# GNN with two residual norms: variances of four node groups on ScalarE, Newton steps a group later, 32 slot lookups moved on GpSimd

## What is computed

```python
# graph attention, 8 heads of 32 features
h = x @ W;  e = leaky_relu(a_src[src] + a_dst[dst], 0.2)
alpha = softmax of e over the edges with the same dst
g = relu(segment_sum(h[src] * alpha, dst) + bias)
x1 = layernorm(x + g)
# three convolutions with a batch norm each
y = x1
for l in range(3):
    e = relu((y[dst] - y[src]) @ theta[l].T + y[src] @ phi[l].T)
    agg = segment_max(e, src), 0 where a node has no edge
    y = relu((agg - mean(agg)) * rsqrt(var(agg) + 1e-5) * gamma[l] + beta[l])
out = layernorm(x1 + y)
```

## Time and profile before

| what | before |
|---|---|
| median of 3 runs | 1826.77 us (1820.73 to 1829.75) |
| the profiled execution, its own time | 1819.43 us |
| its span, first to last instruction | 1817.7 us |
| busy: PE / DVE / ACT / POOL | 1146.8 / 1262.6 / 997.6 / 973.9 us |
| mean granted TensorE clock | 0.811 |
| GAT stage, VectorE, groups 4 to 28 | to 404 us |
| softmax and groups 29 to 39, VectorE | 404 to 537 us |
| message stage and x1 scatters | 537 to 714 us |
| convolution 0, 1, 2 | 714 to 997, 997 to 1255, 1255 to 1460 us |
| last, dense stage | to the end |

### The profile page before, as it was taken

How to read it: one execution, slowest core, us unless ns; L and a number is a source line. 1 busy time by engine, 2 the same in 40 slices (tenths; PEclk the granted TensorE clock), 3 DMA queues, 4 the chain that set the end, 5 groups by cost and what they waited for, 6 DMA issues and landing times.

```text
span 1817.7 us, 16814 instructions
## 1 busy us (share of the span) xinstructions
PE 1146.8 (63%) x3863; PEld 584.4 (32%) x3863; DVE 1262.6 (69%) x2733; ACT 997.6 (55%) x2650; POOL 973.9 (54%) x1032
## 2 busy tenths in 40 slices
PE   0148888870029991899998599997999988000000
PEld 0023333320004441455554355543554444000000
DVE  8847777769979992354544255463766678989998
ACT  4736877765446763334443355553555544756664
POOL 1057767677767667777772777622644237640000
PEclk9999999985555555899999799998999999555555
DMA  9276899987775662688886366865866359999999
GB/s 366 110 219 220 288 330 367 365 273 250 221 283 143 214 208 96 198 258 258 263 260 184 77 180 184 169 171 126 150 130 136 105 160 299 418 402 383 385 378 371
DMA packets 177390, 436.11 MB, mean 240 GB/s; under 512 B 28804, under 2 KB 108810, under 8 KB 157324
## 3 DMA queue, kind: packets, MB, share of 16 engines
q1 hardware_dynamic: 109020, 229.52, 36.1%
q0 software_dynamic: 44800, 100.49, 22.0%
q10 hardware_dynamic: 23472, 105.03, 16.0%
HBM read 257.16 MB, written 182.32 MB: 242 GB/s over the span
## 4 chain that ended last, share of the span: by engine, by line
PE 29%; DVE 22%; DMA 20%; POOL 12%; issue 9%; ACT 7%; SPq 1%; ACTq 0%; POOLq 0%; DVEq 0%
PE ps L1247 10%; PE ps L1260 9%; DMA out<-arena 8%; DMA arena<-x 5%; POOL arena L1199 4%; POOL arena L1218 4%; DVE stat L782 3%; ACT arena L821 3%; DMA x<-big,idx 3%; PE ps L1237 3%; POOL slot L679 3%; PE ps L1424 2%; DVE arena L779 2%; DVE arena L1043 2%; DVE big L1052 2%
## 5 line engine op out<-in xcount | busy, mean ns | idle before, releaser
L1332 DVE TENSOR_TENSOR_SCAN arena<-arena,ps 128x512 f32<-128x512 f32 x150 | 191.0, 1277 | 263.6 <-PE ps L1247 241.8
L836 POOL DMA_INDIRECT arena<-x,idx x200 | 189.7, 948 | 172.7 <-DVE idx L603 90.9
L1218 POOL DMA_INDIRECT arena<-agg,slot x200 | 189.0, 945 | 171.4 <-PE ps L1237 72.3
L1247 PE MATMUL ps<-arena 128*128 128x512 f32 x600 | 277.0, 605 | 3.8 <-DVE arena L1332 3.8
L1260 PE MATMUL ps<-arena 128*128 128x512 f32 x600 | 273.4, 599 | 8.9 <-ACT arena L1302 8.9
L1199 POOL DMA_INDIRECT arena<-x,idx x200 | 189.2, 946 | 62.0 <-issue 58.5
L1529 ACT ACTIVATE ps<-arena 128x256 f32<-128x256 f32 x391 | 143.6, 367 | 100.9 <-DVE arena L1501 100.9
L821 ACT ACTIVATE arena<-arena,shift,inv 128x256 f32<-128x256 f32 (+1 forms) x311 | 156.0, 586 | 51.4 <-DVE shift L813 34.6
L1336 DVE TENSOR_TENSOR ps<-arena,ps 128x512 f32<-128x512 f32 x150 | 103.9, 695 | 107.2 <-PE ps L1260 107.2
L1302 ACT ACTIVATE arena<-big,bn_shift,bn_scale 128x512 f32<-128x512 f32 x100 | 75.9, 806 | 165.1 <-PE ps L1260 154.0
L1260 PEld LDWEIGHTS ps<-arena 128*128 128x128 f32 x600 | 115.2, 192 | 154.1 <-issue 144.7
(11 more groups left out here) (213 smaller groups left out, 2236.2 us busy)
## 6 DMA issues: line engine op xcount, KB each, us to landing
arena<-x SPq DMA_DIRECT2D x39, 1280.0 KB, 9.9
out<-arena SPq DMA_DIRECT2D x39, 1280.0 KB, 12.5
arena<-x ACTq DMA_DIRECT2D x31, 1280.0 KB, 10.5
x<-arena ACTq DMA_DIRECT2D x31, 1280.0 KB, 6.5
agg<-arena SPq DMA_DIRECT2D x50, 512.0 KB, 4.2
arena<-not_same SPq DMA_DIRECT2D x75, 256.0 KB
arena<-last_of SPq DMA_DIRECT2D x75, 256.0 KB
x_dst<-arena SPq DMA_DIRECT2D x25, 512.0 KB, 4.8
```

Of the source, the lines that this page charges most:

```text
L836: pl.indirect_dma_start(rows_in[:, par, a, g, :], None, x[:, :], bass.IndirectOffsetOnAxis(ap=idx[:, k, t * G + g:t * G + g + 1], axis=0)) ...
L1218: pl.indirect_dma_start(conv_in[:, b, 1, g, :], None, agg_dram[l - 1][:, :], bass.IndirectOffsetOnAxis(ap=slot[:, t * G + g:t * G + g + 1] ...
L1247: m = pe.matmul(far_bank[j], thp[:, l, 0, k, j * P:(j + 1) * P], far_t[:, par, k, :], start=(k == 0), stop=(k == 1))
L1332: v.tensor_tensor_scan(runmax[:, par, j, :], mask[:, tl % 2, :], far_bank[j], initial, ALU.add, ALU.max).then_inc(s_conv_scan, 1)
```

## The change

It has three parts. (1) Groups 29, 31, 33 and 35: VectorE no longer takes statistics; `pre_sums` adds the bias row by row with a fused instruction that also gives the row sum (ten instructions and one for the mean), and ScalarE's `pre_squares` takes ten squares of the differences from the mean, with their sums accumulated, into unused PSUM banks, ahead of the root. The other groups, and the tail, keep `pre_stats`. (2) From group 29 on VectorE does the sums or statistics of group g and then the Newton steps of g - 1, and ScalarE the root of g and then the turnover of g - 1. (3) SLOTS_TAIL = 3: only 12 lookups stay in front of the x1 scatters; the 32 others stand behind convolution 0's gathers, before the wait for the aggregates. A doubled definition, of which only the second was in use, goes too.

```diff
--- before.py
+++ after.py
@@ -672,6 +672,7 @@
             s(v.tensor_reduce(tiles_f[:, :], node_end, AX.X, ALU.add))
             s(v.tensor_scalar(tiles_needed[:, :], tiles_f[:, :], 1.0, None, ALU.add))
 
+        SLOTS_TAIL = 3
         SLOTS_EARLY = 11
         SLOTS_STEPS = 7
 
@@ -686,7 +687,7 @@
                 pl.indirect_dma_start(slot_dram[:, :], bass.IndirectOffsetOnAxis(ap=idx[:, S_END, c:c + 1], axis=0),
                                       slot_of_pos[:, c:c + 1], None, bounds_check=N - 1, oob_is_err=False).then_inc(s_slot_put, 16)
             pl.wait_ge(s_slot_put, 16 * NC)
-            for c in range(SLOTS_EARLY * G):
+            for c in range(SLOTS_TAIL * G):
                 slot_lookup(pl, c, s_slot_got)
 
 
@@ -765,11 +766,45 @@
             return 5 * g if g <= PRE_SORT else 5 * PRE_SORT + 4 * (g - PRE_SORT)
 
         def rbias_dve(v):
-            v.wait_ge(s_bias, 16)
-        def rbias_dve(v):
             v.wait_ge(s_rbias, 1)
             v.tensor_copy(rbias_ps, rbias[:, :]).then_inc(s_rbias, 1)
             v.wait_ge(s_rbias, 2)
+
+
+
+        ACT_GROUPS = (PRE_SORT + NS, PRE_SORT + NS + 2, PRE_SORT + NS + 4, PRE_SORT + NS + 6)
+        assert len(ACT_GROUPS) <= PRE_SORT and ACT_GROUPS[-1] < PG
+        unused_bank = (0, 1, 2, 3, 6)
+
+        def mean_and_var(g):
+            rows, p, r = node_rows(g)
+            if g in ACT_GROUPS:
+                k = ACT_GROUPS.index(g)
+                return row_mean[:, k, :], row_var[:, k, :], float(ROOT)
+            return mv[0:p, g % 2, 0:r, 0], mv[0:p, g % 2, 0:r, 1], -1.0
+
+        def pre_sums(v, g):
+            mean, var, scale = mean_and_var(g)
+            c = g - PRE_SORT
+            y = pre_rows(g)
+            loaded(v, g)
+            for n in range(PR):
+                m = v.scalar_tensor_tensor(y[:, n, :], y[:, n, :], 0.0, rbias_ps, ALU.add, ALU.add, accum_out=row_sum[:, n:n + 1])
+                if n == 0:
+                    m.then_inc(s_pre_sum, 1)
+            m.then_inc(s_pre_stat, 1)
+            v.wait_ge(s_pre_stat, c + 1)
+            v.tensor_scalar(mean, row_sum[:, :], -1.0 / (D * ROOT), None, ALU.mult).then_inc(s_pre_mv, 1)
+
+        def pre_squares(a, g):
+            mean, var, scale = mean_and_var(g)
+            k = ACT_GROUPS.index(g)
+            a.wait_ge(s_pre_mv, g - PRE_SORT + 1)
+            for n in range(PR):
+                m = a.activation(bank[unused_bank[n // 2]][:, (n % 2) * D:(n % 2 + 1) * D], pre_rows(g)[:, n, :], ACT.Square,
+                                 scale=1.0 / ROOT, bias=mean[:, n:n + 1], accum_out=var[:, n:n + 1])
+            m.then_inc(s_row_squares, 1)
+            a.wait_ge(s_row_squares, PRE_SORT + k + 1)
 
         def pre_stats(v, g):
             rows, p, r = node_rows(g)
@@ -791,21 +826,25 @@
         def pre_std(a, g):
             rows, p, r = node_rows(g)
             e = g % 2
+            mean, var, scale = mean_and_var(g)
             a.wait_ge(s_pre_mv, g - PRE_SORT + 1)
             a.wait_ge(s_pre_newton, newtons(g - 1))
-            a.activation(std[0:p, e, 0:r], mv[0:p, e, 0:r, 1], ACT.Sqrt, bias=eps_b[0:p, :]).then_inc(s_pre_std, 1)
+            a.activation(std[0:p, e, 0:r], var, ACT.Sqrt, bias=eps_b[0:p, :]).then_inc(s_pre_std, 1)
 
         def pre_finish(v, g):
             rows, p, r = node_rows(g)
             b, e = g % PRE_RING, g % 2
             near, off, d = recip_ps[0:p, 0:r], offset_ps[0:p, 0:r], step[0:p, 0:r]
+            mean, var, scale = mean_and_var(g)
+            if g == PG:
+                v.wait_ge(s_pre_shift, 2 * g)
             v.wait_ge(s_pre_std, g + 1)
             if g >= PRE_RING:
                 v.wait_ge(s_pre_normed, g - PRE_RING + 1)
             v.reciprocal(near, std[0:p, e, 0:r]).then_inc(s_pre_newton, 1)
             v.wait_ge(s_pre_newton, newtons(g) + 1)
-            v.scalar_tensor_tensor(d, mv[0:p, e, 0:r, 1], EPS, near, ALU.add, ALU.mult).then_inc(s_pre_newton, 1)
-            v.scalar_tensor_tensor(off, mv[0:p, e, 0:r, 0], -1.0, near, ALU.mult, ALU.mult).then_inc(s_pre_newton, 1)
+            v.scalar_tensor_tensor(d, var, EPS, near, ALU.add, ALU.mult).then_inc(s_pre_newton, 1)
+            v.scalar_tensor_tensor(off, mean, scale, near, ALU.mult, ALU.mult).then_inc(s_pre_newton, 1)
             v.wait_ge(s_pre_newton, newtons(g) + 2)
             v.scalar_tensor_tensor(d, d, -0.5, near, ALU.mult, ALU.mult).then_inc(s_pre_newton, 1)
             v.wait_ge(s_pre_newton, newtons(g) + 4)
@@ -1200,6 +1239,9 @@
                                               bass.IndirectOffsetOnAxis(ap=idx[:, k, t * G + g:t * G + g + 1], axis=0)).then_inc(got[b], 16)
 
         def later_pool(pl, l):
+            if l == 1:
+                for c in range(SLOTS_TAIL * G, SLOTS_EARLY * G):
+                    slot_lookup(pl, c, s_slot_got)
             pl.wait_ge(s_agg_ready, l)
             if l == 1:
                 pl.wait_ge(s_x1s_ready, 1)
@@ -1588,19 +1630,22 @@
                 rows_square_act(act, g)
             pre_turnover(PRE_SORT - 1)
             act.wait_ge(s_params, PARAMS)
-            for s in range(NS + 2):
+            for s in range(NS + 1):
                 if s < NS:
                     gat_keep(act, s)
                 if 1 <= s <= NS:
                     gat_keep_h(act, s - 1)
                     pre_std(act, PRE_SORT + s - 1)
-                if 2 <= s:
+                if 2 <= s <= NS:
                     pre_turnover(PRE_SORT + s - 2)
             for g in range(EARLY, PG + 1):
                 if g == EARLY + 2:
                     soft_exp_act(act)
+                if g in ACT_GROUPS:
+                    pre_squares(act, g)
                 pre_std(act, g)
-                pre_turnover(g)
+                pre_turnover(g - 1)
+            pre_turnover(PG)
             msg_act(act)
             for l in range(L):
                 conv_act(act, l)
@@ -1629,8 +1674,11 @@
 
             def one_group():
                 nonlocal g
+                if g in ACT_GROUPS:
+                    pre_sums(dve, g)
+                else:
+                    pre_stats(dve, g)
                 pre_finish(dve, g - 1)
-                pre_stats(dve, g)
                 g += 1
             soft_max_1(dve)
             one_group()
```

## The result

The changed kernel takes 1845.98 us (median of 4 runs, 1845.77 to 1848.87), the kernel before beside it 1826.78 (1820.73 to 1829.75). The ratio is 1.0134, 95% interval 1.0110 to 1.0158: **19 us slower by the medians, 20 to 29 by the interval**. The ratio of the two medians alone is 1.0105, under this interval, so the size is known to a few microseconds only. The forecast was 1847.1 and 20.3 us. The profiled execution took 1848.87 us, 29.4 more than that of before: the profiled execution of before was 7.3 us under its median, the changed one 2.9 over its own, and 6.5 us had arisen ahead of VectorE's first edited instruction. So I compare stretches, each from its own start.

The account below looks back on a forecast made before the run. It took VectorE, then the loads' ring of four buffers, to bound the softmax stretch, and GpSimd convolution 1. Loads 9.4, message stage 1.8 and lookups 9.1 sum to 20.3 us: median 1847.1 us, range 1831 to 1858.

Parts of the forecast that it names:

- The lag puts the loads on the path: Softmax stretch: normalisations come later, so loads go out later and VectorE waits for them; message stage starts 9.4 us later.
- Squares at 4.1: ScalarE, softmax stretch: ten squares with accumulator reads take 4.1 us per group, 16.5 us for four groups.
- The exponential fits in the shadow of these loads: Softmax stretch: the exponential and the second squares (31, 33, 35) are hidden behind the waits for loads.
- Load 36 at 11 us: Softmax stretch: load 36 goes out at 497.7, after most message-stage loads, and lands 11 us later, at 508.7.
- about +2: Softmax stretch: the load term if each of four loads took 2 us less, by the Trainium skill's DMA price.
- 9.4 at its quietest: Softmax loads: landing time of a load issued just behind a store around 455 us, held against the skill's price.
- The message stage: Message stage: GpSimd in step from the first tile slows some 9 more VectorE tiles by 0.2 us each, +1.8 us.
- The lookups: Behind convolution 0: 26 of 32 hidden in idle time, six not, plus 2.1 us landing wait; convolution 1 starts 9.1 us later.
- the rival with 1838 us: Convolution 1 absorbs the lookups' excess, the rest as forecast: +11.2 us, 1838 us; chance 0.07.
- Rival 1: Softmax stretch: loads land before VectorE asks, message stage starts 16.6 us earlier; -5.7 us, 1821 us; chance 0.10.
- rival 2: Loads land before VectorE asks and the lookups are hidden too: -14.8 us, 1812 us; chance 0.04.
- Rivals 3 and 5: Softmax loads: four land in 8.1 us each, 1840 us, chance 0.15; two late ones above 15, 1858 up, 0.05.

Follow-up runs that it names:

- the lag alone: Changed kernel without the sums on ScalarE and with the lookups in their old place, against the kernel before: 1.0090, +14.8 us by medians.
- the short loads: Both softmax edits, lookups in their old place, loads of groups 31 and later cut to one row in ten, against the kernel before: 0.9985.
- the two kernels with all edits: The changed kernel, 1845.98 us, and the same with 24 lookups moved, not 32, 1839.76 us.
- the lookups alone: Kernel before with only the 32 lookups moved behind convolution 0's gathers: 1.0072 of the kernel before, +12.7 us by medians.
- the earlier Newton steps: Kernel before with the Newton steps of g-1 ahead of two more softmax pieces on VectorE: 0.9989 of the kernel before, 1821.4 us.

## Why the prediction was right, and where it was off

**The lag puts the loads on the path: right.** The waits that were named are there, ahead of sums(31), sums(33), statistics(36) and (38), and two that were not, ahead of sums(35), 3.2 us, and statistics(37), 2.3; the sum steps end no earlier than before for all the saved VectorE time. Shown by the lag alone (129.8) and by the short loads (115.3).

**Its size was 14.5, not 9.4.** Counted from the end of step one, the forecast's marks and the measured ones (less 6.5) are: load 31 lands 444.5 and 445.3; load 33 lands 468.0 and 470.7; the last sum step ends 484.5 and 487.4; load 36 goes out at 497.7 and 500.6, lands at 508.7 and 514.8; load 38 lands at 532.0 and 537.0; Newton(39) ends at 546.4 and 551.5. Three mis-sized terms make the 5.1 (5.3, less what the other steps came in shorter):
- Squares at 4.1 are 5.05: one takes 0.49 by start to start, where the last stage's take 0.41. The squares of the change have a per-partition bias and those of the last stage have none; no run changes that alone. Two lie on the path: 1.9.
- "The exponential fits in the shadow of these loads": it does, but its table load moved. In the kernel before, the root's table load came at once behind the exponential, at 451.88 (first row below), and VectorE asked for that root only after its scans, at 455.36 (second row). Now squares stand between, without a table load of their own, and the 1.28 us of the load stand between squares and root, on the path. The Trainium skill (ScalarE: Activation LUTs, What ACT_TABLE_LOAD costs) gives about 1283 ns for it, and the row agrees. Its 1.38 us of draining on top aren't seen here: the load starts 0.02 us behind the last square's accumulator read (460.35, 0.18 us), and the root 0.02 us behind the load.
```profile
451.88 1.28 ACT L796 ACT_TABLE_LOAD   x1
```
```profile
455.36 0.20 DVE L805 RECIPROCAL ps<-std 128x10 f32<-128x10 f32 x1
```
- Load 36 at 11 us took 14.2. The reason given, that it goes out after most of the message stage's loads, failed. Load 36 went out 13.2 us behind the last sum step, as worked out. But SP sends its loads only when the store of the alphas has landed, and that took 10.4 us (493.97 to 504.41) where it took 2.9 before, so SP's loads went out from 504.41 on, beside load 36 at 507.12. Nor would the order have helped: in the kernel of the lag alone nearly all of them went out first, from 491.49 to 498.89, and load 36 at 499.43 still took 14.8. Load 38 took 8.9 for 10. Together +2.1.

**The Trainium skill's price for a DMA,** an estimate of 8.0 us with the store, would have taken 1.9, 1.9, 3.0 and 2.0 us off the four loads, so the term by it is +0.6 and not the "about +2" of the prediction. The four took 10.0, 9.7, 14.2 and 8.9. The section (DMA: Bandwidth & Descriptors, Anatomy of one DMA) is on DMAs that GpSimd issues, and these are ScalarE's. "9.4 at its quietest" was misread too: the same rows have 8.1 as the shortest, close to that price. It is the late loads that the price misses: even 0.13 MB took 11.4 us there.

**The message stage: +0.5, not +1.8.** The price per tile held, the number of tiles was wrong. GpSimd's queue in the changed kernel, the first scatter and that of the fourth tile:
```profile
585.68 1.02 POOL L1166 DMA_INDIRECT x<-big,idx  x1 [48.89 <-ACT big L1157]
...
603.43 0.98 POOL L1166 DMA_INDIRECT x<-big,idx  x1 [0.88 <-ACT big L1157]
```
GpSimd stands ready for the first tile, as forecast, and waits for ScalarE at every tile from the fourth on, at 603.43, 45.5 us into the stage; before, such waits set in 69.6 us into it (606.54), four tiles later. The small multiply (now line 1094) takes over 0.3 us on 17 of the 25 tiles, before on 15, and not on nine more. Being under a scatter is not enough to slow it: at 586.15 it took 0.17 us under the one of 585.68. Slow tiles come every 6.16 us and the others every 5.96, so two of them are 0.4 us. The medians, 417 ns for 418, don't show this. Nor is the stage's length a mark of the lookups: the lag alone, with the lookups in their old place, has 20 such tiles and takes 1.0 us more than before, the lookups alone have 18 and take 0.6 more.

**The lookups: +9.0 for +9.1,** landing wait 2.00 for 2.1. Of this term every step held, down to the 43 us. Convolution 1 absorbs none of it, the rival with 1838 us: from its first instruction to that of convolution 2 it takes 257.2 us, 257.6 before.

**Rival 1** (VectorE bound, 1821) fell where it was said to decide, at load 36, and rival 2 with it. Rivals 3 and 5 fell by the four loads' times above: not 8.1 each, and not both late ones over 15. **Open**: the 6.5 us ahead of the edited code. Step one ends at 427.4 and 426.2 in the two kernels with all edits, at 419.7 to 423.4 in the other eight traces of an undisturbed chip. Without it the span's difference would be 22.9. The traces show where it arises, not why: in the GAT stage, which no edit changes. There SP's stores of the gathered rows (`x_dst`) landed as follows between 280 and 380 us, in the changed kernel and in the kernel before:
```profile
DMA to landing us min/median/max: 3.4/12.2/15.0
```
```profile
DMA to landing us min/median/max: 4.8/6.1/8.4
```
In the five traces where step one ends at 422.5 or later this median is 9.3 to 12.2 us, in the other five 5.3 to 6.5. Two of the slow ones have the code of before up to there (the lookups alone, 11.8, and the earlier Newton steps, 10.7), so the edits are not needed for it.

## What to carry to other kernels

Work taken off the busiest engine gained nothing here, because a ring of few buffers stood just behind it. So before delaying what sends out the next load (here a normalisation, behind a root that waited for squares), follow one buffer through its whole round and compare it with what the engine wants. The lag paid where no load hung behind it; here that is the last group alone, and it made the kernel 0.4% quicker. Work moved into an idle stretch costs by what doesn't fit, so count its instructions: 24 fitted, 32 cost 9 us.

## What I had not expected of the hardware

What was already on its way mattered more than a load's own size: 0.13 MB behind a store took 5.3 us while SP was idle, and 11.4 us behind SP's 3.9 MB with the DMA engines full, where the whole 1.31 MB took 9.7 and 14.2. And a function's table load doesn't stay where it was when work that needs no table of its own moves between: 1.28 us went from under VectorE's scans onto the path.
